# LoRA preparation moved between the attention blocks, x loaded once, and the column term on GpSimd, in a cross-attention and LoRA layer

## The reference

```python
def fake_quant(x, scale, zp):
    q = jnp.clip(jnp.round(x / scale + zp), 0.0, 255.0)
    return (q - zp) * scale

x = x + jnp.matmul(fake_quant(layernorm(x), s1, z1), fake_quant(ctx, s2, z2))
y = layernorm(x).reshape(8, 256, 2048)
A_eff = jnp.einsum('bn,nri->bri', gate, lora_A)
B_eff = jnp.einsum('bn,nor->bor', gate, lora_B)
delta = einsum('bor,btr->bto', B_eff, einsum('bri,bti->btr', A_eff, y)) \
      + einsum('or,btr->bto', lora_B_shared, einsum('ri,bti->btr', lora_A_shared, y))
x = x + (matmul(y, kernel) + bias + delta)
```

## Time and profile before

| | us |
|---|---|
| three runs | 1150.94, 1154.97, 1154.24; median 1154.24 |
| the profiled execution | 1151.19 |
| its span, first to last instruction | 1149.6 |
| TensorE busy | 1050.9 (91%) |
| VectorE, ScalarE, GpSimd busy | 615.4, 328.3, 151.1 |
| moved by DMA | 184.15 MB, 160 GB/s on average |

### The profile page before, as it was taken

One profiled execution on the slowest core, in us unless ns is written; L12 is line 12 of the kernel. 1 busy time (PEld: TensorE's weight loads), 2 busy tenths in 40 slices (PEclk: granted clock), 3 DMA queues, 4 the chain that ended last, 5 costly groups with the idle time before them and its releaser, 6 DMA issues.

```text
span 1149.6 us, 12632 instructions
## 1 busy us (share of the span) xinstructions
PE 1050.9 (91%) x4834; PEld 500.0 (43%) x4856; DVE 615.4 (54%) x835; ACT 328.3 (29%) x317; POOL 151.1 (13%) x182
## 2 busy tenths in 40 slices
PE   4976989959999899999999699988999999999996
PEld 3743434424454344444444244434444444444443
DVE  4955787798775545555442587787754114014010
ACT  0766355323221223222221354433223003003000
POOL 1000000020010131231330000010110401301300
PEclk9988989989999999999999799998999999999999
DMA  9799766755775644634679743465673405204001
GB/s 311 188 199 200 283 224 215 293 111 149 141 178 182 203 150 165 189 129 163 199 271 224 247 156 138 146 149 103 134 183 121 143 19 172 75 18 164 9 22 41
DMA packets 197306, 184.15 MB, mean 160 GB/s; under 512 B 139856, under 2 KB 139984, under 8 KB 194768
## 3 DMA queue, kind: packets, MB, share of 16 engines
q1 hardware_dynamic: 166608, 118.05, 37.4%
q0 software_dynamic: 12288, 52.43, 12.9%
q10 hardware_dynamic: 18368, 13.11, 3.9%
HBM read 132.71 MB, written 25.69 MB: 138 GB/s over the span
## 4 chain that ended last, share of the span: by engine, by line
PE 54%; DVE 15%; DMA 14%; ACT 6%; issue 6%; SPq 2%; POOL 2%; ACTq 1%; DVEq 0%; POOLq 0%
PE psum L862 14%; PE psum L960 11%; PE psum L961 11%; PE psum L962 11%; DMA stage<-in_w 4%; DVE stats L1082 3%; DVE ring L1178 2%; DMA xn<-in_x 2%; POOL x L490 2%; DMA bias_sb<-in_bias 2%; ACT ring L601 2%; PE psum L983 2%; DMA sc<-in_z 1%; PE psum L848 1%; DMA x<-in_lora_b 1%
## 5 line engine op out<-in xcount | busy, mean ns | idle before, releaser
L960 PE MATMUL psum<-ring,lhs 128*128 128x512 f16 x1024 | 390.8, 382 | 34.6 <-DVE ring L1178 31.3
L961 PE MATMUL psum<-ring,lhs 128*128 128x512 f16 x1024 | 390.4, 381 | 0.0
L962 PE MATMUL psum<-ring,lhs 128*128 128x512 f16 x1024 | 390.3, 381 | 0.0
L862 PE MATMUL psum<-ring,lhs 128*128 128x512 bf16 x1003 | 234.2, 385 | 16.3 <-DVE ring L1140 14.1
L960 PEld LDWEIGHTS psum<-ring,lhs 128*128 128x128 f16 x1024 | 100.6, 98 | 160.4 <-DVE ring L1178 21.7
L862 PEld LDWEIGHTS psum<-ring,lhs 128*128 128x128 bf16 x1024 | 100.8, 99 | 140.5 <-DVE ring L1140 16.6
L962 PEld LDWEIGHTS psum<-ring,lhs 128*128 128x128 f16 x1024 | 100.7, 98 | 122.6 <-issue 3.1
L961 PEld LDWEIGHTS psum<-ring,lhs 128*128 128x128 f16 x1024 | 100.6, 98 | 120.2 <-issue 2.5
L1233 DVE SCALAR_TENSOR_TENSOR x<-psum,sc,x 128x512 f32<-128x512 f32 (+1 forms) x64 | 45.2, 745 | 188.9 <-PE psum L972 188.1
L601 ACT ACTIVATE ring<-stage,sc 128x2048 f16<-128x2048 f32 x32 | 63.5, 1999 | 209.8 <-PE psum L962 136.3
L490 POOL TENSOR_TENSOR x<-x,bias_sb 128x512 f32<-128x512 f32 (+1 forms) x64 | 87.7, 1396 | 189.5 <-DVE xn L1220 118.9
(11 more groups left out here) (127 smaller groups left out, 760.2 us busy)
## 6 DMA issues: line engine op xcount, KB each, us to landing
stage<-in_w SPq DMA_DIRECT2D x40, 1024.0 KB, 5.9
stage<-in_ctx_in SPq DMA_DIRECT2D x32, 1024.0 KB, 5.2
x<-in_x POOLq DMA_DIRECT2D x8, 2048.0 KB, 9.7
out<-x POOLq DMA_DIRECT2D x64, 256.0 KB, 3.4
xn<-in_x POOLq DMA_DIRECT2D x10, 1024.0 KB, 7.0
x<-in_lora_a SPq DMA_DIRECT2D x4, 1024.0 KB, 19.2
ring<-in_x POOLq DMA_DIRECT2D x4, 1024.0 KB, 9.4
x<-in_lora_b SPq DMA_DIRECT2D x16, 256.0 KB, 4.8
```

Of the source, the lines that this page charges most:

```text
L862: last = pe.matmul(psum[:, t, :], lhs_q[:, k, t * P:(t + 1) * P], ring_q[:, g, j % 2, u, :], start=(k == 0), stop=False)
L960: pe.matmul(psum[:, t, :], hi, ring[:, g, 0, u, :], start=(kk == 0), stop=False)
L961: pe.matmul(psum[:, t, :], hi, ring[:, g, 1, u, :], start=False, stop=False)
L962: last = pe.matmul(psum[:, t, :], lo, ring[:, g, 0, u, :], start=False, stop=False)
```

## The change

The host now stores seven inputs in another layout (a transposition or a reshape, no arithmetic), so that each group of context and weight is one 8 KB row for each of the 128 partitions, and so that LoRA A and B have in partition n x 8 + r the row r of a group of eight rows of LoRA n. One 128-row contraction with a 128 x 64 pattern of the gates gives eight rows for all eight gates.

- *Start.* x's eight tiles are loaded once, all at the beginning, into `x2`; statistics are taken there, and scale and shift are found for two tiles at once (`norm_pair`) and applied in ScalarE's first pass. The normalising pass of VectorE (`norm1`) goes.
- *A* is contracted between attention blocks 0 and 1 (`a_effective`: 64 matmuls of 64 columns, 16 evictions), its peak taken behind block 1's evictions, and in block 2 it is scaled and split into high and low f16 by ScalarE (`gate_hi`) and VectorE (`a_low`), gate by gate in two slots, and stored by GpSimd, 512 KB each. `load_a` later loads that directly to `a_st`.
- *B* is contracted between blocks 2 and 3 (`b_effective`: 16 matmuls of 512 columns), in two buffers of four; its peaks come at the start of block 3. The transpositions of B, and the scratch of the shared B, go.
- *The column term* is copied once by ScalarE, scaled, to f32, and GpSimd adds it to each tile of `x2` behind the row term (`adjust`). The column matmuls and the split go; the very first column sum is 16 matmuls on the groups themselves.
- *Order.* ScalarE has row terms ahead of the context groups. The base phase begins with tiles 0 and 1 together by weight group. SP's load of A waits for the contraction before; peaks of w's block 1 are taken ahead of tile 6.

```diff
-            for t in range(1, TILES):
-                if t >= 4:
-                    pool.wait_ge(q_rows, t - 3)
-                pool.dma_start(x_buf(t), x_tile[0, t]).then_inc(x_in[x_no(t)], 16)
+            for t in range(2, TILES):
+                pool.dma_start(x2[:, t, :], x_tile[0, t]).then_inc(x_in[t], 16)
...
+            sp.wait_ge(x_in[1], 16)
+            load_ctx(0, 0, [0, 1])
+            turn_q(0)
+            turn_q(1)
+            load_ctx(0, 0, [2, 3])
+            turn_q(2)
+            turn_q(3)
+            sp.dma_start(ash, lora_as).then_inc(sh_in, 16)
+            load_lora_a(0)
+            load_lora_a(1)
+            load_ctx(0, 1, [0, 1])
+            for t in range(4, TILES):
+                turn_q(t)
+            load_lora_a(2)
+            load_lora_a(3)
+            load_ctx(0, 1, [2, 3])
+            load_ctx(0, 2, range(NG))
...
             def load_a(b, g):
-                i = grp_a(b, g)
-                sp.wait_ge(converted, i - 1)
-                for n, src in enumerate((b * GPB + g, NGATE)):
-                    sp.dma_start(stage[:, i % 2, n, :].rearrange("p (k r) -> p k r", r=RANK),
-                                 a_scratch[:, src, :, :]).then_inc(stage_in[i % 2], 16)
+                n = b * GPB + g
+                if n:
+                    sp.wait_ge(ax_done, n)
+                sp.dma_start(a_st, a_scratch[n]).then_inc(a_in, 16)
...
                 turn_y(b, 5)
-                load_a(b, 3)
+                if b == 0:
+                    w_peaks_block(1)
                 turn_y(b, 6)
                 turn_y(b, 7)
-                with sp.Fori(1, NBLK) as j:
+                w_block(b, 1, [0, 1])
+                load_a(b, 3)
+                w_block(b, 1, [2, 3])
...
+            def adjust(b, j):
+                n = b * NBLK + j
+                pool.wait_ge(col_ready, n + 1)
+                for t in range(TILES):
+                    pool.wait_ge(with_row, n * TILES + t + 1)
+                    v = x2[:, t, j * NW:(j + 1) * NW]
+                    pool.tensor_tensor(v, v, col_sb[n % 2], ALU.add).then_inc(adjusted, 1)
...
+                    adjust(0, 0)
+                    adjust(0, 1)
+                    largest(1, MX_A, PW_A)
+                    for g in range(NGATE):
+                        pool.wait_ge(a_lo, g + 2)
+                        pool.dma_start(a_scratch[g], a_f16[:, g % 2, :, :]).then_inc(a_dram[g % 2], 16)
+                    adjust(0, 2)
+                    for c in range(NBLK):
+                        pool.wait_ge(be_out, (c + 1) * NQ)
+                        pool.dma_start(bg_rows[:, :, c * NW:(c + 1) * NW], b_buf[c % 2]).then_inc(bg_dram[c % 2], 16)
+                    adjust(0, 3)
...
+            def gate_hi(g):
+                if g >= 2:
+                    act.wait_ge(a_dram[g % 2], 16 * (g // 2))
+                for h in range(2):
+                    last = act.activation(a_f16[:, g % 2, h * KH:(h + 1) * KH, 0:RANK], a_half[h][:, g, :, :], ACT.Copy, scale=SA)
+                last.then_inc(a_hi, 1)
+
+            def b_eff_out(n):
+                c = n // NQ
+                act.wait_ge(be_full, n + 1)
+                if n % NQ == 0:
+                    if c < 2:
+                        act.wait_ge(a_lo, NGATE + 1)
+                    else:
+                        act.wait_ge(bg_dram[c % 2], 16 * (c // 2))
+                        act.wait_ge(peaks, c)
+                act.activation(b_buf[c % 2][:, n % NQ, :], psum[0:GQ, n % 4, :], ACT.Copy).then_inc(be_out, 1)
...
                 for j in range(NBLK):
-                    column_hi(j)
+                    column(j)
+                    row_terms(j)
+                    if b == 0 and j == 2:
+                        shared_hi()
+                        for g in range(NGATE):
+                            gate_hi(g)
                     if j + 1 < NBLK:
                         ctx_block(b, j + 1, [0, 1])
-                    if j == 0:
-                        act.wait_ge(rows_ready, b + 1)
-                    row_terms(j)
+                    if b == 0 and j == 0:
+                        for k in range(KT):
+                            a_eff_out(k)
                     if j + 1 < NBLK:
                         ctx_block(b, j + 1, [2, 3])
+                    if b == 0 and j == 2:
+                        for n in range(NBLK * NQ):
+                            b_eff_out(n)
...
                 if b == 0:
                     first_block()
+                    a_effective()
                 for j in range(0 if b else 1, NBLK):
+                    if b == 0 and j == NBLK - 1:
+                        b_effective()
                     first_by_tile(b, j)
...
             def evict1(b, j, t):
                 dve.wait_ge(psum_full, blk(b, 0, j) * TILES + t + 1)
-                dve.wait_ge(with_row, (b * NBLK + j) * TILES + t + 1)
+                dve.wait_ge(adjusted, (b * NBLK + j) * TILES + t + 1)
...
                 for j in range(NBLK - 1):
+                    if b == 0 and j == 2:
+                        power_a()
+                        a_low()
                     evict_and_convert(b, j)
                     if b == 0 and j == 0:
-                        lora_scales()
+                        peak_a()
                 j = NBLK - 1
-                column_low(b, j)
                 if b == 0:
+                    peaks_b()
                     max_of_w(0, 0)
```

More of the change, by code:

```diff
@@ L34, in build @@
     GU = KT // NG
-    NL, RANK, _ = lora_a.shape
-    NGATE = gate.shape[0]
+    NGATE = gate.shape[1]
+    RANK = lora_bs.shape[0]
+    NQ = lora_a.shape[2]
     GPB = NGATE // NBATCH
@@ new lines, in shared_hi @@
+            def shared_hi():
+                act.wait_ge(a_scale, 1)
+                act.wait_ge(sh_in, 16)
+                for n in range(2):
+                    last = act.activation(a_f16[:, n, :, RANK:R2], ash, ACT.Copy, scale=SA)
+                last.then_inc(a_hi, 1)
[4 more added lines that the diff above has]
+                    last = act.activation(a_f16[:, g % 2, h * KH:(h + 1) * KH, 0:RANK], a_half[h][:, g, :, :], ACT.Copy, scale=SA)
+                last.then_inc(a_hi, 1)
```

772 lines of the change are left out of this document (372 added, 400 removed).

## The result

The changed kernel is slower: 1161.85 us, median of 20 runs (1154.67 to 1179.99), against 1152.16 for 20 runs of the kernel before; ratio 1.0084, 95% interval 1.0061 to 1.0106. The forecast was 1133, with the range ending at 1153. A ratio leaves out the runs that took over 1.5% more than the fastest of their kernel (two of the 20 here, one of the 20 before), and the medians are of all runs. The profiled execution took 1165.81 us, its span is 1164.2, 14.6 more than the 1149.6 before.

A forecast was written before the change was run, and what follows sets the result against it. Winnable time was placed ahead of 257.7 us and in batch 1's turn to base, with waits mostly ended by VectorE's conversions. Terms -14.2 - 0.7 + 3.3 - 7.6 = -19.2 gave 1132.0 or 1135; forecast 1133, range 1103 to 1153.

The forecast's parts named there:

- Start and block 0: Batch 0's beginning: constants land at 10.4, tile 3 is transposed at 46.5, block 0 ends at 78.5.
- rival (d): At the start, the single load of x gains nothing because late tiles hold block 0: +8, 1141; chance 0.08.
- A between blocks 0 and 1: LoRA A's 128 passes in batch 0 at 0.12 us each: 15.4 and a cold microsecond, end at 101.5.
- Term 1: Everything up to batch 0's base phase: it starts at 243.5 instead of 257.7, -14.2 us.
- rival (c): LoRA preparation costs more, A at 0.25 a pass and stores at 7 us: 1151, no change; chance 0.13.
- Scaling and storing A: Gate loop around block 2: rounds of 6.1, stores landing in about 4; TensorE idle from 168.7, evictions from 181.
- B between blocks 2 and 3: LoRA B's 16 contractions in batch 0 take 14.3 us in all; block 3 starts at 202.5.
- First weight block, batch 0: Base phase of batch 0: pauses and A's loads and conversions go, waits are added; -0.7 in all.
- Term 2: From batch 0's base phase start to batch 1: a net -0.7 us.
- Attention, batch 1: Batch 1's attention loop: column matmuls go, but column sums come 30.7 apart against 29.57.
- Term 3: Batch 1's attention: three steps of +1.1, +3.3 us, bounds -6 and +30.
- Rival (a): In each attention block GpSimd's additions serialise with VectorE: +46 over six steps, 1179; chance 0.10.

The follow-up runs named there:

- e11: Changed kernel with the peaks of w's block 1 moved behind tile 7 on SP and `product_p(1)` on VectorE, six executions: 1148.15 us, ratio 0.990 to the kernel before.
- e12: Changed kernel with 32 zero-weight matmuls filling the pause ahead of A: 1150.69 us, ratio 0.994 to the kernel before.
- e9: Changed kernel with the column term back on TensorE, split as in the kernel before, without GpSimd's additions: 1162.38 us, ratio 1.0073 to the kernel before.
- c5: c4 plus 26 zero-weight matmuls ahead of A, context groups 2 and 3 converted behind A's second and ninth evictions: 1126.40 us, ratio 0.963 to the kernel before.
- e1: Same edit of the changed kernel as e11, peaks of w's block 1 moved later, in one single execution: 1144.81 us.
- c6: c5 plus 48 zero-weight matmuls behind batch 0's last attention tile, ahead of the base phase: 1122.17 us, ratio 0.962 to the kernel before.
- e2: Changed kernel with A's 64 contractions over 32 columns instead of 64: A's 128 passes took 27.49 us.
- c4: Changed kernel with w's peaks late, constants, context groups and the turn between blocks 2 and 3 reordered, spare GpSimd additions behind all-reduces: 1130.28 us, ratio 0.981.
- e8: Kernel before with only the host's new layout of context and w: 1156.87 us, ratio 1.0040 to the kernel before.

## Why the prediction was wrong

Two steps turned the sign; either alone is worth more than the 9.7 us between the two medians, since e11 and e12, which mend one each, are both faster than the kernel before. In the prediction's order:

*Start and block 0.* Expected constants at 10.4, bounds 8 and 15; VectorE began at 14.0, statistics at 15.9. With 8 MB of x queued at once the small loads came late, the side of the bound that rival (d) names; tile 3 at 49.7 instead of 46.5, block 0's end near 84.2 instead of 78.5: 5.7 of the miss. The first attention matmul came at 38.5, ahead of the 44 to 50 given as a sign, which won nothing, since tile 3 was late.

***A between blocks 0 and 1*, the step that failed in Term 1.** "I take 0.12: 15.4 and a cold microsecond." The 0.12 is right at a clock of 1.00: e9, e12 and c5 have 14.4 to 14.5. What failed is "a cold microsecond": the pause that the same paragraph works out ahead of A (78.5 to 84.8) lets the clock fall, and it did not rise again during these passes. 27.5 instead of the 16.7 between 84.8 and 101.5: 10.9. The bound of 32 held it, as rival (c) did with 0.25 a pass, but for another reason. The first eviction was 1.7 later than worked out.

The price stood in the trace of before. The earlier trace rows has the nearest row once, at 75.90, where no pause is ahead; the same 16 passes stand there twice more behind pauses:

```profile
64.13 3.65 PE L836 MATMUL psum<-b_st,x 128*128 128x128 f32 x16 [7.17 <-DMA x<-in_lora_b]
106.28 3.67 PE L836 MATMUL psum<-b_st,x 128*128 128x128 f32 x16 [8.29 <-DMA x<-in_lora_b]
```

That is 0.23 a pass, at a granted clock of 0.50, and 128 of those would have made 29 us. What these rows could not tell is how long the level lasts: there the clock was at 1.00 again 4.3 us on (from 110.6), in A it was not after 27.

*Scaling and storing A.* Right: a round of two gates took 5.1 (6.1 expected), a store landed in 2.9 (4 taken). It was put down as the place where the win is given back, and it is, but not by the landing alone: what was queued behind it counts. GpSimd's 7.04 ahead of its additions was seen by no step.

*B between blocks 2 and 3.* 26.8 from first contraction to block 3, 21.5 expected. The passes took 18.4 instead of 14.3, with the first 4 us behind each of the two pauses (11.92 and 7.57) at 0.50; the wait for the buffer and the hand-over were worked out as there, 8.3 instead of 7.2. Together 5.3. With 5.7, 1.7, 10.9 and 5.3, less 0.5 in the stretches between them and by rounding, that is the 23.1 between -14.2 and +8.9.

***First weight block, batch 0*, the step that failed in Term 2.** "Peaks of w's block 1 now stand ahead of tile 6. I trace base tile 6 4.7 late [...] and 0.8 for its product." The place was named and its price missed: it was followed on SP, where w's load is queued behind the wait for A, and not on VectorE, where the second product is queued behind the peaks. Measured 13.5 for that wait, 16 to 18 with what followed it in the profiles of e1 and e11, and 21 (13.7 by the medians) over the whole kernel. The rest of the term came out better than worked out: without the peaks' place the stretch is 8 to 9 shorter than before, not 0.7; which of its parts was mis-sized is open.

*Attention, batch 1* and *Turn to base, batch 1.* Right: column sums 30.05 apart (30.7 forecast), +1.9 for +1.4; -7.2 for -5.7. Rival (a) did not come, though its mechanism is there: 0.35 a conversion. That the two ways take the same time in batch 1 (e9) fits the small positive Term 3.

Of the rivals (c) was nearest, 1151 for preparation that costs more; slower than that needed its A and the wait of Term 2, which no rival had. The side slower by over 0.5% had 0.10, all of it for (a).

## What to carry to other kernels

Where an edit puts work with a load ahead of other work, follow the order of every engine in the chain from the load to TensorE, not only the queue that issues the load; reductions placed ahead of one product turned a gain of 1% into a loss of 0.8%. A pause ahead of TensorE is to be priced at its length and at the clock of what follows it: read the granted clock of the stretch before a pass's duration is carried to another place, look in the trace for the same row behind a pause, and try filling the pause, as e12 did ahead of A. An experiment on a duration is to be made at either clock before it says what the duration is made of. And a part that is taken out changes what stands around it: e9 gave back the column matmuls and, unasked, the clock of A.

## What the runs showed of the hardware

- 128 f32 passes of 64 columns took 27.5 us at a granted clock of 0.50 and 14.4 to 14.5 at 1.00, and in these executions the clock kept its level from the first pass to the last (0.50 behind a pause of 7.9, 1.00 without one). A pause of 1.03 or 0.63 ahead kept it (e12, c5); in c6, with 2.32, it fell after A had begun, and A took 25.9. At 0.50, 32 columns took as long as 64 (e2).
- 16 f32 passes of 128 columns took 3.65 and 3.67 us behind pauses of 7.17 and 8.29, and 1.91 without one (kernel before).
- In attention of batch 0 GpSimd stood 5.6 to 7.5 us at a change between an all-reduce and additions (11.7 to 12.1 at the first spare addition of c4, c5 and c6); a spare addition took that off the path.
- Two transpositions by DMA ahead of batch 1 took 7.19 us in one execution (e1) and 16.10 in another of the same kernel (e11), 11.39 in the changed kernel, 8.59 and 23.41 in the kernel before and in e8. TensorE's wait there was 0.1 to 0.3 less each time: 6.89, 15.80, 11.09, 8.29 and 23.28. What the transpositions wait for is open.
